# A gated FFN's down projection on one Trainium2 core: block products for the first quad of each turned group as well, and four slots for the tiles of sums

## What is computed

```python
x = x + attention(layernorm(x), ctx)            # one head, 256 wide
h = layernorm(x)                                # 1792 rows
g = einsum('bsh,ehf->ebsf', h, w_gate)          # 8 experts, F = 1024
u = einsum('bsh,ehf->ebsf', h, w_up)
y = einsum('ebsf,efh->ebsh', silu(g) * u, w_down)
x = x + einsum('ebsh,bse->bsh', y, cw)          # all 8 experts, weighted per row
```

## Time and profile before

| | |
|---|---|
| time, median of 3 runs | 947.73 us (947.09 to 948.34) |
| the profiled execution: time, span | 949.7 us, 947.8 us |
| PE busy, share of the span | 941.7 us, 99% |
| PE weight loads | 874.2 us, 92% |
| POOL, ACT, DVE busy | 714.2, 672.9, 653.6 us (75%, 71%, 69%) |
| matmuls recorded | 5007 |
| TensorE clock granted | 1.000 of full speed |

### The profile page before, as it was taken

How to read it: one execution, slowest core, us unless ns; L and a number is a source line. 1 busy time by engine, 2 the same in 40 slices (tenths; PEclk the granted TensorE clock), 3 DMA queues, 4 the chain that set the end, 5 groups by cost and what they waited for, 6 DMA issues and landing times.

```text
span 947.8 us, 15935 instructions
## 1 busy us (share of the span) xinstructions
PE 941.7 (99%) x5007; PEld 874.2 (92%) x5007; DVE 653.6 (69%) x1248; ACT 672.9 (71%) x1347; POOL 714.2 (75%) x662
## 2 busy tenths in 40 slices
PE   9999999999999999999999999999999999999998
PEld 7999899999999999999999999999999999999998
DVE  4898444665767767677767677667777776776764
ACT  5998556677777776877777777778777776777662
POOL 4899986687778686777777786877777777868565
PEclk9999999999999999999999999999999999999999
DMA  7473331230101110020101120111101120112026
GB/s 195 133 167 84 98 96 24 102 100 26 64 24 45 43 64 23 23 65 14 56 19 45 43 65 24 45 43 42 45 3 43 43 65 23 45 42 73 10 40 156
DMA packets 73241, 55.92 MB, mean 59 GB/s; under 512 B 30244, under 2 KB 69485, under 8 KB 73158
## 3 DMA queue, kind: packets, MB, share of 16 engines
q1 hardware_dynamic: 73150, 54.91, 19.9%
q10 hardware_dynamic: 8, 0.00, 0.0%
HBM read 46.58 MB, written 6.48 MB: 56 GB/s over the span
## 4 chain that ended last, share of the span: by engine, by line
PE 96%; issue 1%; POOL 1%; ACT 1%; DVE 1%; DMA 1%; SPq 0%; POOLq 0%; DVEq 0%; ACTq 0%
PE ps L405 94%; PE ps L2533 1%; DMA xf<-in_L_xattn_Wk 1%; PE ps L2569 0%; POOL w_raw L898 0%; POOL arena L749 0%; PE ps L2521 0%; PE ps L2586 0%; DVE early L1820 0%; ACT arena L1051 0%; PE ps L2612 0%; PE ps L2479 0%; ACT xf L1059 0%; POOLq L110 0%; ACT xf L1051 0%
## 5 line engine op out<-in xcount | busy, mean ns | idle before, releaser
L405 PE MATMUL ps<-xc_hi,w_hi 128*128 128x448 f32 x904 | 330.7, 366 | 0.0
L405 PE MATMUL ps<-xc_lo,w_hi 128*128 128x448 f32 x904 | 330.2, 365 | 0.0
L405 PE MATMUL ps<-xc_hi,w_lo 128*128 128x448 f32 x904 | 330.2, 365 | 0.0
L405 PE MATMUL ps<-arena 128*128 128x448 f32 (+5 forms) x1644 | 309.5, 332 | 0.2 <-DVE arena L416 0.2
L749 POOL TENSOR_TENSOR arena<-shared,arena 128x448 fp32r<-128x448 f32 x196 | 225.4, 1158 | 75.6 <-ACT arena L1359 71.7
L405 PEld LDWEIGHTS ps<-arena 128*128 128x128 f32 (+2 forms) x1644 | 264.5, 186 | 14.6 <-DVE arena L416 0.4
L405 PEld LDWEIGHTS ps<-xc_hi,w_hi 128*128 128x128 f32 x904 | 169.8, 188 | 13.6 <-ACT ps L1289 0.2
L405 PEld LDWEIGHTS ps<-xc_hi,w_lo 128*128 128x128 f32 x904 | 169.8, 188 | 13.6
L405 PEld LDWEIGHTS ps<-xc_lo,w_hi 128*128 128x128 f32 x904 | 169.8, 188 | 13.2
L1955 DVE TENSOR_TENSOR shared<-shared,ps 128x448 f32<-128x448 f32 x60 | 37.1, 619 | 109.0 <-ACT shared L1338 69.3
L738 POOL TENSOR_TENSOR w_lo<-w_raw,w_hi 128x1792 fp32r<-128x1792 f32 (+1 forms) x17 | 66.0, 3882 | 60.7 <-ACT w_hi L1167 60.7
(11 more groups left out here) (209 smaller groups left out, 1562.9 us busy)
## 6 DMA issues: line engine op xcount, KB each, us to landing
early<-in_L_ffn_w_down SPq DMA_DIRECT2D x16, 512.0 KB, 3.8
xf<-cw_dram SPq DMA_DIRECT2D x16, 448.0 KB, 4.6
shared<-in_ctx SPq DMA_DIRECT2D x16, 336.0 KB
w_raw<-in_L_ffn_w_gate SPq DMA_DIRECT2D x17, 256.0 KB, 2.7
w_raw<-in_L_ffn_w_up SPq DMA_DIRECT2D x17, 256.0 KB, 3.4
early<-in_L_ffn_w_gate SPq DMA_DIRECT2D x15, 256.0 KB, 2.7
early<-in_L_ffn_w_up SPq DMA_DIRECT2D x15, 256.0 KB, 3.0
xsacc<-in_x SPq DMA_DIRECT2D x8, 224.0 KB, 6.3
```

The source lines that it names most:

```text
L405: ins = nc.tensor.matmul(dst, w, m, start=first and i == 0, stop=last and i == len(passes) - 1, skip_group_check=onto)
```

## The change

The first quad of a turned group also goes in seven products. `down_1` to `down_7` now each hold the products of both quads, accumulated in the same bank: six matmuls of 448 columns. `whole_part` and `down_last` are gone, and a turned group has seven steps in `unit_ready` instead of eight. For that:

- `t1` to `t4`, their high and low parts run for every quad of a turned group (they now take a quad `n`, not a group), and HID12 of first quads is no longer split;
- the weight sums are 128x2x128, for both quads at once;
- `up_5(n)` waits for `t4(n-1)` and `high_t2(n-1)` after every turned quad;
- turned quads take three of the four slots of `hs` in turn (`slot`), and each hidden tile waits for the step that read that part of the slot last; the fourth slot holds sums and their parts; other sums lie in the ends of the slots and in three older rooms;
- `down_c22` waits for the copy `SEED_X` instead of the eighth step; `turn_cw` stands earlier; two memsets at the start count on `consts_set`, for which PE waits to 4 instead of 2;
- all four engines' lists are written anew.

```diff
+    OF_PLAIN = (1, 0, 2)
-    DP1, DC11, DP6, DP5, DC12, DP7, DC21, DC22 = range(1, 9)
+    DP1, DC11, DP6, DP7, DP5, DC12, DC21 = range(1, 8)
         def strassen_quad(n):
-            return n % FPAIRS == 1 and n // FPAIRS in TURNED
+            return n // FPAIRS in TURNED
+        def slot(n):
+            if n < PLAIN:
+                return n
+            if n == QUADS - 3:
+                return 3
+            return OF_PLAIN[(n - PLAIN - (n > QUADS - 3)) % 3] if n < QUADS - 2 else {QUADS - 2: 1, QUADS - 1: 0}[n]
...
             def sum_s1_s3(hn):
-                nc.gpsimd.tensor_tensor(s_raw[:], wd_raw[:, 2, P:2 * P], wd_raw[:, 3, P:2 * P], ALU.add).then_inc(s_made, 1)
+                nc.gpsimd.tensor_tensor(s_raw[:], wd_1[1], wd_2[1], ALU.add).then_inc(s_made, 1)
...
             def up_5(n):
                 if n > PLAIN and strassen_quad(n - 1):
-                    i = n // FPAIRS - 1 - CP
-                    pe.wait_ge(t_made, 6 * i + MADE4)
-                    pe.wait_ge(t_hi_done, 4 * i + HIGH2)
+                    pe.wait_ge(t_made, 6 * (n - 1 - PLAIN) + MADE4)
+                    pe.wait_ge(t_hi_done, 2 * (n - 1 - PLAIN) + HIGH2)
...
-            def whole_part(g, k):
-                c, block = k // 2, slice(k % 2 * P, (k % 2 + 1) * P)
-                h, toks = hs[FPAIRS * g % HSLOTS], slice(c * TC, (c + 1) * TC)
-                return [x for j in range(2) for x in three(wd[:, 0, 1 - j, block], wd[:, 1, 1 - j, block], h[:, 0, j, toks], h[:, 1, j, toks])]
+            def by_hidden(g, t, j, c):
+                return [x for p in range(FPAIRS) for x in three(*down_block(2 * p + t, 0), *hidden_of(FPAIRS * g + p, j, c))]
+            def by_sum(g, t, k):
+                return [x for p in range(FPAIRS) for x in three(*down_block(2 * p + t, 1), t_hi[p][k], t_lo[p][k])]
+            def sum_by_sum(g, s, k):
+                return [x for p in range(FPAIRS) for x in three(s_hi[s][:, p, :], s_lo[s][:, p, :], t_hi[p][k], t_lo[p][k])]
             def down_1(g):
-                accumulate(ps_unit[0], three(*down_block(2, 0), *hidden_of(g, 1, 1))).then_inc(unit_ready, 1)
+                accumulate(ps_unit[0], by_hidden(g, 0, 1, 1)).then_inc(unit_ready, 1)
             def down_2(g):
-                accumulate(ps_unit[0], three(*down_block(3, 0), *hidden_of(g, 0, 1)) + whole_part(g, 2),
-                           first=False, onto=True).then_inc(unit_ready, 1)
+                accumulate(ps_unit[0], by_hidden(g, 1, 0, 1), first=False, onto=True).then_inc(unit_ready, 1)
...
-            def down_last(g):
-                accumulate(ps_unit[1], whole_part(g, 1), first=False, onto=True).then_inc(unit_ready, 1)
```

More of the change, by code:

```diff
@@ L1609, in opening @@
                 gate_seed(m)
+                high_set(2 * hn + 1)
+                gate_keep5(m)
+                gate_keep2(m)
+                high_part(1, 's13')
+                up_seed(m)
+                up_keep2(m)
+                activate11(m)
+                activate(m, g22[0], C22_SUM)
+                activate(m, g12[0], C12_SUM)
+                up_keep5(m)
+                activate21(m)
+                high_hidden(m, HID11, g11, 0, 0)
+                gate_seed(m + 1)
+                high_part(1, 's2')
@@ new lines, in opening @@
+                activate(m + 1, g12[1], C12_SUM)
+                activate21(m + 1)
+                high_hidden(m + 1, HID11, g11, 0, 0)
+                high_hidden(m + 1, HID22, g22[1], 1, TC)
+                gate_seed(m + 2)
+                high_t4(m)
+                high_t3(m + 1)
+                high_down(hn)
+                up_seed(m + 2)
+                gate_keep5(m + 2)
+                gate_keep2(m + 2)
+                high_t2(m + 1)
+                up_keep2(m + 2)
+                activate11(m + 2)
@@ new lines, in opening @@
+                high_t1(m + 1)
+                high_hidden(m + 1, HID21, g21, 0, TC)
+                up_keep5(m + 2)
+                high_s(hn, 1)
+                high_hidden(m + 2, HID11, g11, 0, 0)
+                activate(m + 2, g22[0], C22_SUM)
+                activate(m + 2, g12[0], C12_SUM)
+                high_t4(m + 1)
+                high_hidden(m + 2, HID22, g22[0], 1, TC)
+                down_seed_y(g + 1)
+                activate21(m + 2)
+                gate_seed(m + 3)
@@ new lines, in opening @@
+                high_set(2 * hn + 2)
+                down_keep2(g + 1)
+                high_s(hn, 2)
+                gate_keep5(m + 3)
+                gate_keep2(m + 3)
+                high_t3(m + 2)
+                up_seed(m + 3)
+                down_keep5(g + 1)
+                high_t1(m + 2)
+                high_t2(m + 2)
+                up_keep2(m + 3)
+                high_hidden(m + 2, HID21, g21, 0, TC)
+                activate11(m + 3)
+                high_hidden(m + 3, HID11, g11, 0, 0)
@@ L3074, in opening @@
                 up_1(m)
+                turn_cw()
                 gate_5(m)
```

913 lines of the change are left out of this document (450 added, 463 removed).

## The result

The changed kernel took 940.58 us (median of 5 runs, 939.06 to 942.64) beside 947.73 for the kernel before: 0.9928 of its time, 95% interval 0.991 to 0.9946. It is faster by 7.2 us where 16.8 were forecast, and 940.6 lies above the range. The profiled execution of after took 939.91 us.

A forecast was written before the change was run, and what follows sets the result against it. PE was taken as the bound, a round being nothing but its matmuls. From the profiled 949.7: less 17.0 for matmuls, plus 0.5 stalls, less 0.3 at the end, 932.9; less 2.0 gives a median of 930.9, range 929.3 to 933 (8 in 10: to 938).

The forecast's parts named there:

- The count: Turned groups: 42 matmuls instead of 45 in 28 groups, 84 fewer of 448 columns, worth 17.0 us.
- The load of the vector engines: Per round of 51.06 us: DVE busy 44.8, ACT 42.2, POOL 43.9 us, costing nothing while PE covers them.
- No PE wait in the rounds: Walk of `four` found no place where PE must wait, four with little left; 0.5 us taken for stalls.
- the slow rival: `up_5` waits for the T chain after each of 56 quads; if 1.2 us late, 34 us lost, 965; chance 0.05.
- the rival of engines that can't keep the round: Three vector engines at 83 to 88% hold rounds near 52.2 us, gain lost: 942 to 948; chance 0.05.
- The end: Program's close: the last turn chain no longer ends the run, PE's last products do; 0.3 us gained.
- 0.2026 us each: Price of one 448-column matmul in gate, up and down; a removed one gives back its whole slot.
- The tell-tale: Sign that the forecast is wrong: a round over 51.4 us, or a matmul distance that is not 0.2026.
- the walk: Step-by-step timing of the new list for `four`; four tight places, 0.13 to 0.5 us left.
- The rival of small waits: Small PE waits in every round at the tight places: 0.3 us in 14 rounds, 4.2 us, 935; chance 0.20.

The follow-up runs named there:

- e1: The changed kernel once more, nothing edited; 940.91 us, 0.9928 of the kernel before.
- e5: Changed kernel with one ScalarE exchange in the middle rounds: the second quad's seed ahead of the HID11 cast; 942.5 us.
- e3: Changed kernel with six VectorE operations in first quads of turned groups cut to 8 of 448 columns; 940.77 us.
- e12: Changed kernel plus a 64-column matmul ahead of gate_1 of the fourth quad in each middle round; 935.27 us.
- e13: e12 with the opening's up_keep5 of the first turned quad one place earlier in ScalarE's list, ahead of the Silu of g12; 932.09 us.
- e11: e4 with the cast of the down weights in two halves, one on each side of the third quad's seed, in the middle rounds; 942.15 us.
- e2: Changed kernel with low parts of weights, down-weight sums and hidden rows made zeros, all instructions kept; 940.18 us.
- e4: Changed kernel with three ScalarE copies each moved one place in the middle rounds' list; 935.67 us.
- e6: Kernel before, with the up seed of each odd quad copied in two halves of 224 columns; 961.86 us.
- e7: e6 plus one 64-column matmul ahead of gate_1 of the first quad in each middle round; 949.04 us.
- e15: e11 plus a 64-column matmul ahead of gate_1 of the fourth quad in each middle round; 935.61 us.
- e14: Changed kernel plus a 64-column matmul ahead of gate_1 of the third quad in each middle round; 938.37 us.
- e8: Kernel before plus one 64-column matmul ahead of gate_1 of the first quad in each middle round; 948.76 us.
- e10: e4 with the down cast behind both kept gate products, plus a 64-column matmul ahead of the third quad's gate_1; 966.28 us.

## Why the prediction was wrong

**The count** held: 84 matmuls, 17.0 us. **The load of the vector engines** held within 1.5 us: 43.3, 41.8 and 43.7 us a round against 44.8, 42.2 and 43.9. **No PE wait in the rounds** held in every profile of the changed kernel; the 0.5 us set aside for it was not used. (That a wait "cannot be a gain" is not so here: by e1 and e5 a load that comes just late can bring the narrow spacing back.) `up_5`, the slow rival's place, never waited, and the rival of engines that can't keep the round did not come: e3 took work away and gained nothing. **The end** went as walked: PE's last product, then `add_rows`, no longer `add_back` on POOL. Behind PE's end came 3.4 us before (944.39 to 947.8) and 2.7 after, 0.7 less where 0.3 was taken.

```profile
935.44 0.02 issue
935.47 0.48 DVE w_raw L2028
```

**The step that failed** is "0.2026 us each", the price of a matmul read from the kernel before and carried over to the new one. It is the price of one of two spacings. By the spacing of after's profile 500 us cost 9.7 us more; the 0.5 that before had is in the earlier trace rows as well, so the sum is off by 9.2. The tell-tale was named ("wrong if a round is over 51.4 us, or if the matmul distance is not 0.2026"), but as a mishap without a chance or a mechanism, since none of the rows read from before shows that a distance can change at the same clock. Its timeline from 109 to 135 us would have: there its own matmuls are 0.2067 apart, as shown above.

**The second** is small: the walk covered `four` and not `opening`, where `up_keep5` stands behind a Silu that waits for a slow VectorE operation (4.47 us at L1940). 1.4 us.

Together, on medians: 930.9 + 9.2 + 1.4 - 0.5 = 941.0; less the 0.4 by which the end gave more than forecast it is 940.6, and 940.58 was measured. (That the two agree so closely is in part luck: the executions of after spread over 3.6 us.) A closer test leaves out the start of the program, which differs by 3 us between executions: from the 901st recorded matmul to the last, before took 808.39 us. Less 17.0, plus wide stretches, opening wait and extra matmuls as each profile has them, that gives 802.4 for after, 797.6 for e12 and 795.6 for e13; their traces read 802.27, 797.82 and 795.65. Nothing of size is left.

**The rival of small waits** (0.20, 935) had the right places and the wrong currency. The semaphores at `gate_6(m+1)`, `gate_6(m+2)` and `gate_7(m)`, with 0.13 to 0.2 us left by the walk, did come just late; PE lost nothing at them directly. What they do is seen in the spacing: with the one at `gate_6(m+1)` gone, nothing ended the wide stretches (e5). That one of them starts a wide stretch is seen only by its place; e11 went wide without any.

**Shown:** two spacings with the same instructions, waits and clock; that they stay with zeros in a third or more of the products (e2) and with most of VectorE's added load gone (e3); that the order and length of ScalarE's copies (e4, e5, e6) and a narrow matmul on TensorE (e7, e12, e15) change which one holds, and a move of the latter where a wide stretch begins (e14); that the wide one is reachable from the kernel before (e6). **Not shown:** what has the two patterns, inside TensorE or in what it shares with others, what starts a wide stretch, and a rule for which way a given nudge goes. "Phase" is a name for it here, not a finding.

## What to carry to other kernels

On a kernel that TensorE bounds with no waits, check the start-to-start distance of the matmuls along the whole program, not once: equal work, equal clock and no wait can still differ by 2%. If a harmless edit on another engine costs 1 to 2%, look for this before a cause in the edit, and try one narrow matmul a round, at several places: of the six kernels that were run here with and without one four were faster by it (e7, e12, e14, e15), one lost its bare cost (e8) and one 5.0 us (e10). And walk the opening and closing lists as well as the loop.

## What was not expected of the hardware

- A matmul of 448 columns came every 202.7 or every 206.7 ns at granted clock 1.00, on one core. In the wide spacing single distances are 206 or 207 ns; in the narrow one they go round in five steps, near 203, 202, 199, 207, 202. The Trainium skill ("TensorE: Matmul & The Clock Gate", Back-to-back issue gap) gives N/2.4 + 2.5 ns for the isolated gap, as an estimate 189 ns here, and about 131 ns for 512 columns in a sustained stream. The traces agree with neither, and show two values for one width.
- The spacing is kept until something tips it: for 759 us in e6 (172 to 931), over some 3,700 matmuls by 0.2067 us each.
- Matmuls of 256 columns came every 120 ns in the mean ahead of a wide stretch and ahead of a narrow one (e6 and before, at 166 to 174 us).
- A matmul of 64 columns put into the stream cost 0.11 us (rounds of 52.39 us in e8 against 52.28 before).
